# Two graph layers on one core: layer 1's mask and maximum in two pieces, one load for both graphs' target scores, and x asked for behind it

## What is computed

```python
# layer 0
h = einsum('bnd,ade->bane', x, W)                      # 12 heads of 64
th = tanh(h)
attn_src = einsum('bane,aeo->bano', th, w_src)         # one number for each node and head
attn_dst = einsum('bane,aeo->bano', th, w_dst)
attn = attn_src + swapaxes(attn_dst, 2, 3)             # source's score + target's score
attn = where(attn >= 0, attn, 0.2 * attn)              # leaky rectifier
attn = softmax(where(~adj, -999.0, attn), axis=-1)
feat = elu(einsum('banm,bame->bane', attn, h) + b)
gate = sigmoid(x @ H_w.T + H_b)
x = layernorm(x + gate * feat + (1 - gate) * x)
# layer 1: six-headed attention inside each graph with Wq, Wk, Wv, Wf, the same mask, layernorm
```

## Time and profile before

| | |
|---|---|
| median of 3 runs (lowest, highest) | 2755.78 us (2752.92, 2757.6) |
| the profiled execution's own time | 2753.85 us |
| its span in the trace | 2752.1 us, granted TensorE clock 0.998 |
| TensorE matmul busy | 2723.5 us, 99% of the span |
| VectorE, ScalarE, POOL busy | 61%, 44%, 34% |
| VectorE up to 915 us (the first layer) | 803.0 of 915 us |
| chain that ended last | PE 88%, DVE 6%, DMA 2%, issue 2%, ACT 1% |

### The profile page before, as it was taken

How to read it: one execution, slowest core, us unless ns; L and a number is a source line. 1 busy time by engine, 2 the same in 40 slices (tenths; PEclk the granted TensorE clock), 3 DMA queues, 4 the chain that set the end, 5 groups by cost and what they waited for, 6 DMA issues and landing times.

```text
span 2752.1 us, 51889 instructions
## 1 busy us (share of the span) xinstructions
PE 2723.5 (99%) x20988; PEld 2516.5 (91%) x20988; DVE 1679.9 (61%) x3335; ACT 1211.6 (44%) x3109; POOL 926.7 (34%) x566
## 2 busy tenths in 40 slices
PE   8999999999999989999999999999999999999998
PEld 7777878888878889999999999999999999999998
DVE  7899998888888664444445444444545444444543
ACT  5666676666666633323332333323333333233332
POOL 2353334443444123323333233323332333323330
PEclk9999999999999999999999999999999999999999
DMA  6655665555555521222222222222222222222220
GB/s 183 172 138 145 168 161 135 145 138 141 143 137 138 169 75 58 82 70 81 59 69 71 82 70 58 81 79 73 59 71 72 79 70 63 77 82 70 59 70 24
DMA packets 306895, 269.50 MB, mean 98 GB/s; under 512 B 227808, under 2 KB 244192, under 8 KB 306656
## 3 DMA queue, kind: packets, MB, share of 16 engines
q1 hardware_dynamic: 306656, 266.19, 35.3%
HBM read 142.65 MB, written 75.89 MB: 79 GB/s over the span
## 4 chain that ended last, share of the span: by engine, by line
PE 88%; DVE 6%; DMA 2%; issue 2%; ACT 1%; POOL 0%; SPq 0%; DVEq 0%; ACTq 0%; POOLq 0%
PE ps_hg L1057 22%; PE ps_k L70 15%; PE ps_a L1232 15%; PE ps_a L70 14%; PE ps_q L70 14%; PE ps_s L1173 2%; PE ps_c L1198 2%; PE ps_pv L1089 1%; DMA dst_all<-dst_scratch 1%; PE ps_t L1076 1%; PE ps_pt L1198 1%; ACT logits L563 1%; DMA dst_scratch<-dst 1%; PE ps_pt L1180 1%; DVE logits L787 1%
## 5 line engine op out<-in xcount | busy, mean ns | idle before, releaser
L1057 PE MATMUL ps_hg<-w_hi,xT 128*128 128x512 f32 x2268 | 745.3, 401 | 3.0 <-DVE h_one L820 2.7
L1057 PEld LDWEIGHTS ps_hg<-w_hi,xT 128*128 128x128 f32 x2268 | 426.2, 188 | 106.2 <-issue 4.8
L1057 PE MATMUL ps_hg<-w_lo,xT 128*128 128x512 f32 x1134 | 448.5, 395 | 0.0
L70 PE MATMUL ps_k<-x1T_hi,wk_hi 128*128 128x256 f32 x1152 | 329.0, 286 | 0.0
L70 PE MATMUL ps_k<-x1T_lo,wk_hi 128*128 128x256 f32 x1152 | 321.8, 279 | 0.0
L70 PE MATMUL ps_k<-x1T_hi,wk_lo 128*128 128x256 f32 x1152 | 321.1, 279 | 0.0
L70 PE MATMUL ps_q<-x1T_hi,wq_hi 128*128 128x256 f32 x1140 | 319.3, 280 | 0.0
L70 PE MATMUL ps_q<-x1T_lo,wq_hi 128*128 128x256 f32 x1140 | 318.5, 279 | 0.0
L70 PE MATMUL ps_q<-x1T_hi,wq_lo 128*128 128x256 f32 x1140 | 317.8, 279 | 0.0
L653 ACT ACTIVATE qT<-ps_q,bq_col 128x256 f32<-128x256 f32 x192 | 80.7, 471 | 456.8 <-PE ps_q L70 456.7
L495 POOL TENSOR_TENSOR th_src<-th,wsrc_all 128x768 f32<-128x768 f32 x64 | 118.3, 1849 | 476.9 <-DVE dst_all L800 459.4
(11 more groups left out here) (156 smaller groups left out, 5755.3 us busy)
## 6 DMA issues: line engine op xcount, KB each, us to landing
x_tok<-x SPq DMA_DIRECT2D x64, 384.0 KB, 4.1
dst_all<-dst_scratch SPq DMA_DIRECT2D x128, 192.0 KB, 3.4
gate_scratch<-gate SPq DMA_DIRECT2D x64, 384.0 KB, 2.6
feat_scratch<-feat SPq DMA_DIRECT2D x128, 192.0 KB, 2.8
feat_in<-feat_scratch SPq DMA_DIRECT2D x62, 384.0 KB, 3.1
gate_in<-gate_scratch SPq DMA_DIRECT2D x62, 384.0 KB, 3.8
x_even<-x SPq DMA_DIRECT2D x16, 768.0 KB, 4.2
x_odd<-x SPq DMA_DIRECT2D x16, 768.0 KB, 4.4
```

What stands on the lines that cost most here:

```text
L70: ins = pe.matmul(out, left[a][c], right[b][c], start=(n == 0), stop=(n == len(terms) - 1))
L1057: ins = pe.matmul(ps_hg[:, cols], left[a][c], right[b][c], start=(c == 0 and n == 0), stop=(c == KC - 1 and n == 2))
```

## The change

Three edits, all in the first layer.

1. `spread_dst` loads both graphs' scores with one DMA. Its destination is all 128 rows of `dst_all`; its source is written as a pattern of 2 graphs, each repeated for 64 rows, each 768 numbers long. `dst_in` counts 16 for a tile and not 32.
2. In SyncE's turn `spread_dst(T)` stands ahead of `load_x(T + 3)` and `load_adj(T + 2)`.
3. `softmax_scores` masks and takes the maximum in two pieces (`masked_max`): heads 8 to 11, which VectorE computed itself, before it waits for ScalarE's rectifier, and heads 0 to 7 behind that wait.

```diff
-                for g in range(2):
-                    sp.dma_start(dst_all[graph(g), :],
-                                 dst_rows[T % 2][g * D:(g + 1) * D].partition_broadcast(NODES)).then_inc(dst_in, 16)
+                both = dst_rows[T % 2].rearrange("(g f) -> g f", g=2).unsqueeze(1).to_broadcast([2, NODES, D])
+                sp.dma_start(dst_all[:, :], both).then_inc(dst_in, 16)
...
                 if TURNED <= T + 2 < NT:
                     turn_x(T + 2)
-                    if T + 3 < NT:
-                        load_x(T + 3)
+                spread_dst(T)
+                if TURNED <= T + 2 and T + 3 < NT:
+                    load_x(T + 3)
                 if T + 2 < NT:
                     sp.wait_ge(mask_done, T + 1)
                     load_adj(T + 2)
-                spread_dst(T)
...
+            def masked_max(T, part, first, last):
+                n = last - first
+                scores_ = per_head(logits[:, first * NODES:last * NODES], n)
+                dve.copy_predicated(
+                    scores_, not_adj[:, T % 2, :].unsqueeze(1).to_broadcast([P, n, NODES]),
+                    masked[:, 0:1].unsqueeze(2).to_broadcast([P, n, NODES])).then_inc(masked_done, 1)
+                dve.wait_ge(masked_done, 2 * T + part + 1)
+                dve.tensor_reduce(neg_max[:, first:last], scores_, AX_X, ALU.max, negate=True).then_inc(max_done, 1)
...
-                dve.wait_ge(prelu_done, T + 1)
                 dve.wait_ge(leaky_done, T + 1)
                 dve.wait_ge(mask_done, T + 1)
-                dve.copy_predicated(
-                    per_head(logits[:, :], HEADS0),
-                    not_adj[:, T % 2, :].unsqueeze(1).to_broadcast([P, HEADS0, NODES]),
-                    masked[:, 0:1].unsqueeze(2).to_broadcast([P, HEADS0, NODES])).then_inc(masked_done, 1)
-                dve.wait_ge(masked_done, T + 1)
-                dve.tensor_reduce(neg_max[:, :], per_head(logits[:, :], HEADS0), AX_X, ALU.max,
-                                  negate=True).then_inc(max_done, 1)
-                dve.wait_ge(max_done, T + 1)
+                masked_max(T, 0, ON_ACT, HEADS0)
+                dve.wait_ge(prelu_done, T + 1)
+                masked_max(T, 1, 0, ON_ACT)
+                dve.wait_ge(max_done, 2 * (T + 1))
```

More of the change, by code:

```diff
@@ L556, in leaky_scores @@
             def leaky_scores(T):
-                act.wait_ge(dst_in, 32 * (T + 1))
+                act.wait_ge(dst_in, 16 * (T + 1))
                 act.wait_ge(src_done, T + 1)
@@ L584, in mask_of @@
                 if T >= 2:
-                    act.wait_ge(masked_done, T - 1)
+                    act.wait_ge(masked_done, 2 * (T - 1))
                 act.activation(not_adj[:, T % 2, :], adj_u8[:, T % 4, :], ACT.Copy, scale=-1.0, bias=1.0).then_inc(mask_done, 1)
@@ L770, in rest_x @@
                                       xT[:, T % 2, 0, :, :].bitcast(F32), ALU.subtract).then_inc(lo_done, 1)
+            def masked_max(T, part, first, last):
[6 more added lines that the diff above has]
+                dve.tensor_reduce(neg_max[:, first:last], scores_, AX_X, ALU.max, negate=True).then_inc(max_done, 1)
             def softmax_scores(T):
-                dve.wait_ge(dst_in, 32 * (T + 1))
+                dve.wait_ge(dst_in, 16 * (T + 1))
                 dve.wait_ge(src_done, T + 1)
```

## The result

The changed kernel takes 3051.31 us, the median of 4 executions (3049.01 to 3052.01), against 2755.64 us of the kernel before on the same chip: 1.1074 of its time, with an interval of [1.1057, 1.109]. It is slower by 295.7 us. The profiled execution took 3049.01 us, its span is 3047.3.

The account below looks back on a forecast made before the run. TensorE, busy 99% of the span, bounds the kernel; the slowed target-score loop would exceed its 14.31 us a tile. 63 rounds add 287 us, the layers' border 4: 2753.85 + 291 = 3045 us, range 2955 to 3160.

Parts of the forecast that it names:

- Two engines carry the single load: Spreading load: cut by the source's outermost count of 2, it uses two DMA engines and 14 stand idle; chance 0.76.
- The price of the landing: Spreading load on two engines, issue to landing: 10.0 us against 4.01 before, ends 9.2 and 10.7.
- The store's wait: Small store of `dst`, with x behind the spreading: 1.9 us, ends 1.4 and 2.9, where tile 21 took 3.25.
- the round of 18.9: Target-score loop, first layer: store, spreading, rectifiers and next `dst` take 18.9 us a tile, against TensorE's 14.31.
- The other two links: Target-score loop: 2.58 us to the rectifiers' end, then 4.40 to the next `dst`, where it was 4.94.
- Between the layers: End of the first layer: the last tile's scores come 6 us later, of which about 4 may show.
- TensorE's clock: TensorE in the first layer: a lower clock for some microseconds is covered by its wait of 4.6 us a tile.
- third rival: Two engines and TensorE's clock at the lower level throughout: 28.6 us a tile, 3655 us; chance 0.03.
- Both cost nothing: First layer: x landing later, just in time, and the adjacency, needed a tile later, cost nothing when pushed back.
- the big term: First layer: 63 rounds slowed by the two-engine load take 1191 us and not 904.2, +287.
- second rival: With 16 engines, POOL's split of x falls on the loop's last operations: 2785 us; chance 0.04.
- first rival: All 16 engines carry the single load: a round falls to 12.9 us, 2750 us in all, not slower; chance 0.15.

Follow-up runs that it names:

- experiment 2: The kernel before with the single load for both graphs alone, x still loaded ahead of the store: 3115.93 us, 1.1303 of the kernel before.
- experiment 1: The changed kernel with two half loads again in place of the single load, new order and pieces kept: 2755.87 us, 0.9999 of the kernel before.
- experiment 10: Changed kernel with two half loads, and POOL's split of x waiting until VectorE finished its own heads' rectifier: 2750.36 us, 0.998 of the kernel before.

## Why the prediction was right, step by step

**Two engines carry the single load.** Right, and it alone makes the slowness: experiment 2 has it without the rest, experiment 1 the rest without it, and the time follows the outermost count of the source from 2 over 4 and 8 to 16, with the share of working engines at 0.13, about 0.25 and 0.50 for the first three. The Trainium skill, "DMA: Bandwidth & Descriptors", section "Why a DMA increments its semaphore by 16 and not by 1" (the engines used are the largest number up to 16 that divides the slowest count of both sides), agrees with these shares and with the order of the four times.

**The price of the landing.** 10.0 us taken, 10.42 and 10.51 measured: inside its ends, and just at the "7.8 + 2.6 = 10.4" that the prediction worked out first and then took less than. Of the difference, x's load behind it can explain about 0.3 us: experiment 2, with x ahead, has 10.12.

**The store's wait.** The one link of the round sized wrong by more than a tenth: 1.9 us taken from ends of 1.4 and 2.9, 1.45 to 1.49 measured. With x behind it, it fell to the lower end, the value of tile 63 with nothing in front. Too much here and too little for the landing cancelled, so the round of 18.9 met 19.0 by luck in part.

**The other two links.** 2.58 us to the end of the rectifiers and 4.38 (4.40) to the next `dst` came as worked out. The pieces cost and save what was estimated: 0.51 + 0.80 us for the mask and 0.42 + 0.69 for the maximum, against 1.09 and 0.95 whole, so a fixed part of about 0.15 to 0.2 us each, taken as 0.1 to 0.3. One step was wrong in small: VectorE should no longer wait for the rectifiers, but the first piece ends before they do, and a wait of about 0.5 us a tile is left, 30 us in all.

**Between the layers.** +4 us taken; about 1.6 were measured for all that lies behind the last store. The untouched second layer alone differs by more between two traces (3 us in experiment 10), so this term was not shown either way.

**TensorE's clock.** It did fall after waits, to a mean of 0.66 in the window shown, a part of it at the lower level of 1.2 GHz, and to 0.93 over the first layer. The round is fully explained by its four links without it, so the wait covered it, as the prediction said of its third rival. TensorE's busy share in the first layer was 83% and not 76%, and this fits: the matmuls are as many as before, and count 2822.5 - 2723.5 = 99 us more busy time. So of the 4.6 us of waiting forecast for a tile, about 3.1 were waiting (198 us in all) and about 1.5 went into matmuls that took longer. What a lower clock would cost without such a wait, no run measured.

**"Both cost nothing"**, said of x and the adjacency pushed back. This step failed, though the big term hid it. With two half loads the split of x falls on VectorE's first two passes of the loop and takes 0.82 us a tile from them, and x's load behind the halves lengthens their landing, by 0.8 us in the tiles where ScalarE waited (5.0 against 4.2) and by 0.4 over all tiles (4.6 against 4.1). That eats the 0.54 us of the pieces and the 0.7 of the shorter store wait (median 2.15 before, 1.43 in experiment 1). The split is what decided it: experiment 10 has the longer landing too (5.1 us) and gains all the same. It is the mechanism of the second rival at another place: that rival put the split on the last operations of the loop. For the same reason the 2750 us of the first rival did not come with 16 engines: 2756.42 and 2755.87 us, until the split was moved (2750.36, tried with the two half loads alone). A smaller step of the same paragraph failed in the changed kernel: x was to land some 4 us after its issue and took 10.7. There it cost nothing, since the round had room for it. The Trainium skill, "SBUF — State Buffer", section "Who interferes with whom", which the prediction cited for the port that both engines share, agrees with the 1.72 us beside the split against 0.43 without.

## What to carry to other kernels

When two transfers are merged into one, look at the outermost count of each side as it is written, the source's too: a broadcast of two sources has 2 there, and here that cost 10.4 us instead of 4.2, in a loop that the whole layer hung on. What mends it here with the right output is one load for each source; the single load with 16 outermost read other nodes' scores and only served to show the cause. A load that is moved moves what its landing triggers; ask on which instruction of the neighbouring engine that now falls. And where a loop just keeps pace with the engine that bounds the kernel, a microsecond lost counts 63 times and a microsecond gained hardly at all.

## What the runs showed that I had not expected

- A load of 384 KB asked for right behind the spreading delays it: by 1.0 us where it runs on 4 engines (7.9 against 6.9) or 8 (6.1 against 5.1), by 0.3 where it runs on 2, by 0.8 where two halves run on all 16 (5.0 against 4.2, in the tiles where ScalarE waited).
- A masked copy and a maximum over 256 columns took 0.52 and 0.42 us beside POOL's split (experiment 10), and 0.51 and 0.42 in the mean of experiment 1, where the split has mostly ended by then; a pass that multiplies and takes a maximum was held to 1.72 us. Not every operation of VectorE is held by POOL.
